# A mixer stage whose per-head reciprocal roots are made on all channels by one block-diagonal matrix

## The chip, the cores and the metric

The kernel runs on one core of a Trainium2 chip. The metric is the time of one execution on the device, in microseconds (us), less being better. The engines named below are TensorE (PE, with PEld for its weight loads), VectorE (DVE), ScalarE (ACT), GpSimd (POOL) and SyncE (SP), which issues the DMAs.

## The reference, cut to what matters

The whole network is four layers on an input of 8 x 512 x 256 in fp32: a mixer with an MLP, a mixture of experts, a gated delta attention and an expert-choice selection. The change touches only the mixer, in which each head of 16 channels is divided by its root mean square:

```python
def _rms(x, eps):
    return x * jax.lax.rsqrt(jnp.mean(x * x, axis=-1, keepdims=True) + eps)

q, k, v, a, g = jnp.split(x @ in_proj_w.T, 5, axis=-1)   # each reshaped to (B, S, 16 heads, 16)
q = _rms(q, EPS_FP32)
...
y = gate * (q * memory) + (1.0 - gate) * v               # memory: a decaying scan over k*v
return y.reshape(B, S, D) @ out_proj_w.T
...
x = x + RES_SCALE * _mixer(h1, in_proj_w, out_proj_w)
h2 = norm2_w * _rms(x, 1e-06)
return x + RES_SCALE * (jax.nn.silu(h2 @ fc_w.T) @ proj_w.T)
```

## The kernel before

The four stages follow one another; each has its own block, which begins when the one before has ended. The mixer, `stage_mixer`, works on one batch element (512 tokens x 256 channels) at a time. Channels are held on partitions in two halves (`KT` = 2), so a full tile is `[128, 2, 512]`, which the profile calls 128x1024; token-major tiles are `[128, 4, 256]`.

The loop is a hand-written software pipeline over `steps`: in one step each engine works on batch b (its attention half) and on batch a = b - 1 (its MLP half). The order in which each engine takes its pieces is written out by hand, and semaphores join them. Step 0 has no a, and the ninth step has no b.

PE in one step: `turn_h(b)` (L169, transposes), `project(b, 0, 6)` (L180), `turn_h2(a)` (L218), `project(b, 6, 10)`, `sum_heads(b)` (L189), `widen(a)` (L227, the MLP's first product), `spread_heads(b)` (L197 and L201), `narrow(a)` (L236, its second product), `project_out(b)` (L208).

DVE in one step: `second_norm(a)` (L402 to L409), `states(b)` (L362 to L374), `layer_norm(b + 1)` (L339 to L355), `head_norm(b)` (L381 and the shared helper `rsqrt`, L65 to L70), `mix(b)` (L388 to L393), `finish(a)` (L418).

ACT evicts PSUM: `scale_h` (L267), `parts` (L276 for the squares `q2`, L279 for the five projections), `squares` (L284), `scale_h2` (L289), `hidden` (L294), and last in a step the copy of the turned roots to `rqT` (L313). POOL adds `resm` (L321).

The roots of one batch take this path before the change. `sum_heads` makes the sums of squares per token and head by 8 products, in which slices of `q2` are the weights and the 16-column `head_sum` streams through; the result is 128 x 64 in PSUM bank 0. `head_norm` scales them and runs `rsqrt`, a bit trick with two integer operations and three Newton steps of three operations, on 128x64. `spread_heads` turns the roots to 16 x 512 (L197), ACT copies them to SBUF (L313), and two products with `head_spread` (L201) give each channel its root in banks 2 and 3. `mix` reads those in its first product (L388), and writes `y`, on which `project_out` waits.

Of the kernel before, what the change touches and what calls it, by code (L numbers as in the profile page):

```python
# [10 lines left out]
ALU = mybir.AluOpType  # L11
ACT = mybir.ActivationFunctionType
AX = mybir.AxisListType

P = 128
BATCH = 8
SEQ = 512
DIM = 256
KT = DIM // P
TT = SEQ // P  # L20
# [42 lines left out]
def rsqrt(eng, link, y, v, t):  # L63

    link(eng.tensor_scalar(t.bitcast(I32), v.bitcast(I32), 1, None, ALU.logical_shift_right))  # L65
    link(eng.tensor_scalar(y.bitcast(I32), t.bitcast(I32), -1.0, float(0x5F3759DF), ALU.mult, ALU.add))
    for step in range(3):
        link(eng.scalar_tensor_tensor(out=t, in0=y, scalar=-0.5, in1=y, op0=ALU.mult, op1=ALU.mult))
        link(eng.tensor_tensor(t, t, v, ALU.mult))
        last = eng.scalar_tensor_tensor(out=y, in0=t, scalar=1.5, in1=y, op0=ALU.add, op1=ALU.mult)  # L70
        if step < 2:
            link(last)
    return last
# [3 lines left out]
def stage_mixer(nc, io, x_in, x_out):  # L77
    HEADS, HDIM, CHUNK = 16, 16, 64
# [5 lines left out]
    Q_EPS = float(np.finfo(np.float32).eps)  # L84
# [5 lines left out]
    with ctx:  # L90
# [6 lines left out]
        n1 = sb("n1", [P, KT])  # L97
        n2 = sb("n2", [P, KT])
        ident = sb("ident", [P, P])
        head_sum = sb("head_sum", [P, KT, HEADS])  # L100
        head_spread = sb("head_spread", [HEADS, DIM])
        xin = sb("xin", [P, 3, TT, DIM])
        z = sb("z", [P, 2, TT, DIM])
        h = sb("h", [P, TT, DIM])
# [10 lines left out]
        prefix = sb("prefix", [P, KT, SEQ])  # L115
        mem = sb("mem", [P, KT, SEQ])
        y = sb("y", [P, KT, SEQ])
        rqT = sb("rqT", [HEADS, SEQ])
        hid = sb("hid", [P, FT, SEQ])
        sq = sb("sq", [P, TT, DIM])  # L120
        stats = sb("stats", [P, TT, 6])
# [1 line left out]
        rstd, r1, r2 = sb("rstd", [P, TT]), sb("r1", [P, TT]), sb("r2", [P, TT])  # L123
        vv, tmp, v2, tmp2 = (sb(n, [P, TT]) for n in ("vv", "tmp", "v2", "tmp2"))
        ss = sb("ss", [P, TT])
        rq, qv, tq = (sb(n, [P, TT * HEADS]) for n in ("rq", "qv", "tq"))
        two = sb("two", [P, 1])
        pace = sb("pace", [P, 1])
        ps = ctx.enter_context(nc.psum_tensor("mx_ps", [P, 8, 512], F32))
        names = ("w_in_loaded w_loaded x0 x1 x2 const_set h hTp hT proj proj_out q2 qs rq rqTp rqT rb y op mid ss resm h2 h2Tp h2T "  # L130
                 "fc hid mo out stored dv_norm dv_mem dv_q dv_y dv_h2").split()
        s = {n: sem(n) for n in names}
        x_sem = (s["x0"], s["x1"], s["x2"])
        W_IN_LOADS, W_LOADS = 3, 6
        block = ctx.enter_context(nc.Block())
        tok = lambda x, b: x[b].rearrange("(t p) d -> p t d", p=P)
        steps = [(b - 1 if b else None, b if b < BATCH else None) for b in range(BATCH + 1)]
# [1 line left out]
        @block.sync  # L139
        def _(sp):  # L140
            sp.dma_start(xin[:, 0, :, :], tok(x_in, 0)).then_inc(s["x0"], 16)
            for dst, src in [(ident[:, :], io["ident"]), (n1[:, :], io["norm1_w"]),
                             (w_in[:, :, :], io["in_projT"].rearrange("(k p) n -> p k n", p=P))]:
                sp.dma_start(dst, src).then_inc(s["w_in_loaded"], 16)
            sp.dma_start(xin[:, 1, :, :], tok(x_in, 1)).then_inc(s["x1"], 16)
            for dst, src in [(head_sum[:, :, :], io["head_sum"].rearrange("(k p) n -> p k n", p=P)),
                             (head_spread[:, :], io["head_spread"]), (n2[:, :], io["norm2_w"]),
                             (w_out[:, :, :], io["out_projT"].rearrange("(k p) n -> p k n", p=P)),
                             (w_fc[:, :, :], io["fcT"].rearrange("(k p) n -> p k n", p=P)),
                             (w_proj[:, :, :], io["projT"].rearrange("(k p) n -> p k n", p=P))]:  # L150
                sp.dma_start(dst, src).then_inc(s["w_loaded"], 16)
            sp.dma_start(xin[:, 2, :, :], tok(x_in, 2)).then_inc(s["x2"], 16)
            for b in range(BATCH):
                if b + 3 < BATCH:
                    sp.wait_ge(s["resm"], b + 1)
                    sp.dma_start(xin[:, b % 3, :, :], tok(x_in, b + 3)).then_inc(x_sem[b % 3], 16)
                sp.wait_ge(s["out"], b + 1)
                sp.dma_start(tok(x_out, b), outb[:, :, :]).then_inc(s["stored"], 16)
            sp.wait_ge(s["stored"], 16 * BATCH)

        @block.tensor
        def _(pe):
# [20 lines left out]

            def sum_heads(b):
                pe.wait_ge(s["q2"], KT * b + KT)
                pe.wait_ge(s["proj_out"], b * PARTS + 7)
                for t in range(TT):
                    for k in range(KT):
                        m = pe.matmul(ps[:, 0, t * HEADS:(t + 1) * HEADS], q2[:, k, t * P:(t + 1) * P],  # L189
                                      head_sum[:, k, :], start=(k == 0), stop=(k == KT - 1))  # L190
                m.then_inc(s["qs"], 1)

            def spread_heads(b):
                pe.wait_ge(s["proj_out"], b * PARTS + PARTS)
                pe.wait_ge(s["rq"], b + 1)
                for t in range(TT):
                    m = pe.transpose(ps[0:HEADS, 1, t * P:(t + 1) * P], rq[:, t * HEADS:(t + 1) * HEADS], ident[:, :])  # L197
                m.then_inc(s["rqTp"], 1)
                pe.wait_ge(s["rqT"], b + 1)
                for k in range(KT):  # L200
                    m = pe.matmul(ps[:, 2 + k, :], head_spread[:, k * P:(k + 1) * P], rqT[:, :], start=True, stop=True)  # L201
                m.then_inc(s["rb"], 1)

            def project_out(b):
                pe.wait_ge(s["y"], b + 1)
# [34 lines left out]
            for a, b in steps:  # L240
                if b is not None:
                    turn_h(b), project(b, 0, 6)
                if a is not None:
                    turn_h2(a)
                if b is not None:
                    project(b, 6, PARTS)
                    if b == 0:
                        pe.wait_ge(s["w_loaded"], 16 * W_LOADS)
                    sum_heads(b)
                if a is not None:  # L250
                    widen(a)
                if b is not None:
                    spread_heads(b)
                if a is not None:
                    narrow(a)
                if b is not None:
                    project_out(b)

        @block.scalar
        def _(act):  # L260
# [35 lines left out]
            for a, b in steps:  # L296
                if b is not None:
                    scale_h(b)
                if a is not None:
                    squares(a)  # L300
                if b is not None:
                    parts(b, 0, 6)
                if a is not None:
                    if a == 0:
                        act.wait_ge(s["w_loaded"], 16 * W_LOADS)
                    scale_h2(a)
                if b is not None:
                    parts(b, 6, PARTS)
                if a is not None:
                    hidden(a)  # L310
                if b is not None:
                    act.wait_ge(s["rqTp"], b + 1)
                    act.activation(rqT[:, :], ps[0:HEADS, 1, :], ACT.Copy).then_inc(s["rqT"], 1)  # L313

        @block.gpsimd
        def _(pool):
# [7 lines left out]
        def _(dve):  # L324
# [2 lines left out]
            dve.wait_ge(s["const_set"], 2)  # L327
            norm = Chain(dve, s["dv_norm"], 38)
            memory = Chain(dve, s["dv_mem"], 7)
            qnorm = Chain(dve, s["dv_q"], 11)  # L330
            gated = Chain(dve, s["dv_y"], 4)
            mid = Chain(dve, s["dv_h2"], 12)

# [44 lines left out]
            def head_norm(b):  # L378
                qnorm.start(b)
                dve.wait_ge(s["qs"], b + 1)  # L380
                qnorm(dve.tensor_scalar(qv[:, :], ps[:, 0, 0:TT * HEADS], 1.0 / HDIM, Q_EPS, ALU.mult, ALU.add))  # L381
                rsqrt(dve, qnorm, rq[:, :], qv[:, :], tq[:, :]).then_inc(s["rq"], 1)
                qnorm.end()

            def mix(b):
                gated.start(b)
                dve.wait_ge(s["rb"], b + 1)
                gated(dve.tensor_tensor(y[:, :, :], ch[Q][:, :, :], ps[:, 2:4, :], ALU.mult))  # L388
                gated(dve.tensor_tensor(y[:, :, :], y[:, :, :], mem[:, :, :], ALU.mult))
                gated(dve.tensor_tensor(y[:, :, :], y[:, :, :], ch[V][:, :, :], ALU.subtract))  # L390
                dve.wait_ge(s["proj_out"], b * PARTS + PARTS)
                gated(dve.tensor_tensor(y[:, :, :], y[:, :, :], ch[G][:, :, :], ALU.mult))
                dve.tensor_tensor(y[:, :, :], y[:, :, :], ch[V][:, :, :], ALU.add).then_inc(s["y"], 1)  # L393
                gated.end()
# [1922 lines left out]
def shape_constants():  # L2317

    f = np.float32
    head_sum = np.zeros((DIM, 16), f)  # L2320
    head_sum[np.arange(DIM), np.arange(DIM) // 16] = 1
    row, col = np.arange(P)[:, None], np.arange(P)[None, :]
    masks = np.zeros((P, 7, P), f)
    for l in range(7):
# [5 lines left out]
    for t in range(TT):  # L2330
# [5 lines left out]
    ident = np.eye(P, dtype=f)  # L2336
    krow = np.zeros((P, 1), f)
    krow[::32] = -1
    return dict(ident=ident, head_sum=head_sum, head_spread=head_sum.T, iota8=rows(8), masks=masks,
                keep128=keep128, ident4=np.broadcast_to(ident[:, None, :], (P, 4, P)), ones=np.ones((P, 1), f),  # L2340
                iota256=rows(SEQ // 2), before=before,
                lower=lower, krow=krow, keep_e=keep_e.reshape(P, -1), iota_b=rows(71))
# [40 lines left out]
```

## Time and profile before

| what | us |
|---|---|
| median of 3 runs | 4057.43 (4054.55 to 4061.96) |
| profiled execution, whole time | 4019.23 |
| its span | 4017.4 |
| PE busy in the span | 3306.8 (82%) |
| DVE busy | 2361.9 (59%) |
| ACT busy | 1368.9 (34%) |
| mixer, to its last store | 0 to about 514 |

The profiled execution is one execution, and every start and duration quoted below is of it. "Busy" counts the time in which an engine executes; the clock column is the clock granted to TensorE as a share of full speed, so 1.00 is 2.4 GHz and 0.50 is 1.2 GHz. An fp32 matmul of the program stands in the profile as two matmul instructions.

### The profile page before, as it was taken

What the parts mean: (1) busy time and instruction counts of PE and PEld (TensorE: products, weight loads), DVE (VectorE), ACT (ScalarE), POOL (GpSimd) and SP (SyncE); (2) the same over time, 40 slices, a digit from 0 to 9 for tenths busy, and PEclk for the clock granted to TensorE, in tenths of its full rate; (3) what the DMA queues carried; (4) which work ended last, traced back from release to release, by engine and by line L of the source; (5) the groups of instructions that cost most, each with busy time, mean ns of one, the idle gap of its engine ahead of it and who ended that gap; (6) DMA issues with size and microseconds to landing.
All of it is one profiled execution on the core that took longest, in us unless ns stands there. A gap on an engine that the chain in (4) does not pass through costs nothing. (4 is left out here: it accounts for less than half of the span.)

```text
span 4017.4 us, 53883 instructions
## 1 busy us (share of the span) xinstructions
PE 3306.8 (82%) x18986; PEld 2568.6 (64%) x18986; DVE 2361.9 (59%) x6068; ACT 1368.9 (34%) x2745; POOL 152.0 (4%) x149
## 2 busy tenths in 40 slices
PE   6999958888999999033698989898989889578777
PEld 3665534456999999022486868677676779455454
DVE  5555235545777777354668676766768584344442
ACT  2323212222444444000444453535344443022232
POOL 0000000023000000600000000000000000000000
PEclk8999969998999999555788889797979796578787
DMA  1000040024898987411201011010110100100000
GB/s 59 21 16 11 11 149 11 11 86 178 320 319 321 320 319 274 133 44 52 72 33 33 33 33 35 30 38 28 41 46 19 54 16 7 51 11 11 22 17 11
DMA packets 200529, 331.11 MB, mean 82 GB/s; under 512 B 29665, under 2 KB 154618, under 8 KB 199106
## 3 DMA queue, kind: packets, MB, share of 16 engines
q1 hardware_dynamic: 194114, 310.80, 22.3%
q0 software_dynamic: 6144, 16.79, 1.3%
q8 instruction: 159, 2.61, 0.3%
q14 instruction: 112, 0.92, 0.1%
HBM read 279.17 MB, written 48.37 MB: 82 GB/s over the span
## 5 line engine op out<-in xcount | busy, mean ns | idle before, releaser
L719 PE MATMUL ex_ps<-ex_xbT,ex_w 128*128 128x128 f32 x4544 | 532.4, 276 | 0.5 <-issue 0.5
L719 PEld LDWEIGHTS ex_ps<-ex_xbT,ex_w 128*128 128x128 f32 x4544 | 526.0, 193 | 4.5 <-issue 0.9
L1355 PE MATMUL de_ps<-de_hT,de_w 128*128 128x512 f32 x640 | 307.6, 639 | 26.4 <-DMA de_w<-in_w_kqv_dram 12.6
L799 ACT ACTIVATE ex_t<-ex_ps,ex_b 128x128 f32<-128x128 f32 x568 | 208.9, 368 | 336.5 <-PE ex_ps L719 320.0
L1355 PEld LDWEIGHTS de_ps<-de_hT,de_w 128*128 128x128 f32 x640 | 129.5, 207 | 187.7 <-issue 185.7
L663 PE MATMUL ex_ps<-ex_xT,ex_w 128*128 128x512 f32 x512 | 231.0, 607 | 14.6 <-DVE ex_gl L876 11.4
L876 DVE SCALAR_TENSOR_TENSOR ex_gl<-ex_ps,ex_b,ex_t 128x128 f32<-128x128 f32 (+1 forms) x316 | 123.6, 391 | 142.4 <-ACT ex_t L799 76.7
L663 PEld LDWEIGHTS ex_ps<-ex_xT,ex_w 128*128 128x128 f32 x512 | 97.6, 194 | 133.4 <-issue 113.6
L1712 DVE SCALAR_TENSOR_TENSOR de_ya<-de_kx,de_taps,de_ya 128x512 f32<-128x512 f32 x192 | 142.4, 750 | 49.8 <-ACT de_ya L1551 45.2
L876 DVE SCALAR_TENSOR_TENSOR ex_gm<-ex_ps,ex_b,ex_t 128x128 f32<-128x128 f32 (+1 forms) x316 | 121.7, 385 | 58.1 <-ACT ex_t L772 44.6
L180 PE MATMUL mx_ps<-mx_hT,mx_w_in 128*128 128x512 f32 x320 | 143.2, 604 | 8.3 <-ACT mx_hT L267 8.3
L1712 DVE SCALAR_TENSOR_TENSOR de_ya<-de_qx,de_taps,de_ya 128x512 f32<-128x512 f32 x192 | 142.8, 751 | 8.8 <-ACT de_ya L1551 2.6
L731 PE MATMUL ex_ps<-ex_w,ex_hid 128*128 128x256 f32 x568 | 134.5, 380 | 1.8 <-DVE ex_hid L901 1.8
L1076 PE MATMUL ga_ps<-ga_ident,ga_h 128*128 128x128 f32 x64 | 15.8, 427 | 143.2 <-DVE ga_h L1137 143.2
L1462 PE MATMUL de_ps<-de_PQ,de_DG 64*128 64x64 f32 x512 | 112.7, 417 | 16.6 <-ACT de_PQ L1615 16.6
L236 PE MATMUL mx_ps<-mx_w_proj,mx_hid 128*128 128x256 f32 x512 | 124.3, 408 | 0.0
L1462 PEld LDWEIGHTS de_ps<-de_PQ,de_DG 64*128 64x128 f32 x512 | 109.7, 327 | 20.4 <-ACT de_PQ L1615 20.4
L236 PEld LDWEIGHTS mx_ps<-mx_w_proj,mx_hid 128*128 128x128 f32 x512 | 105.0, 206 | 22.1 <-issue 5.8
L227 PE MATMUL mx_ps<-mx_h2T,mx_w_fc 128*128 128x512 f32 x256 | 114.7, 607 | 0.8 <-ACT mx_h2T L289 0.8
L2217 DVE TENSOR_REDUCE se_M<-se_ps 128x4 f32<-128x1024 f32 x64 | 75.3, 1219 | 65.9 <-PE se_ps L1981 65.7
L180 PEld LDWEIGHTS mx_ps<-mx_hT,mx_w_in 128*128 128x128 f32 x320 | 60.5, 193 | 81.4 <-issue 67.2
L898 DVE SCALAR_TENSOR_TENSOR ex_gl<-ex_gl,ex_gm 128x128 f32<-128x128 f32 (+1 forms) x316 | 105.4, 334 | 11.1 <-DVE ex_gl L896 0.2
(382 smaller groups left out, 6368.2 us busy)
## 6 DMA issues: line engine op xcount, KB each, us to landing
ex_w<-in_w_all_dram SPq DMA_DIRECT2D x144, 1024.0 KB, 7.1
ex_w<-in_w_all_dram SPq DMA_DIRECT2D x72, 512.0 KB, 7.9
de_w<-in_w_kqv_dram SPq DMA_DIRECT2D x80, 256.0 KB, 2.8
de_ab<-alpha_d SPq DMA_DIRECT2D x8, 2048.0 KB, 8.4
ex_xs_d<-ex_yb SPq DMA_DIRECT2D x71, 128.0 KB, 1.9
ex_xb<-ex_xs_d SPq DMA_DIRECT2D x71, 128.0 KB, 7.3
ex_ys_d<-ex_yb SPq DMA_DIRECT2D x71, 128.0 KB, 7.3
mx_xin<-in_x_dram SPq DMA_DIRECT2D x8, 512.0 KB, 3.9
```

The lines of the kernel that those rows point to most:

```text
L180: m = pe.matmul(ps[:, (n + 2) % 4, :], w_in[:, k, part * DIM + half * P:part * DIM + (half + 1) * P], hT[:, k, :], start=(k == 0), stop=(k ...
L227: m = pe.matmul(ps[:, 4 + f % 2, :], w_fc[:, k, f * P:(f + 1) * P], h2T[:, k, :], start=(k == 0), stop=(k == KT - 1))
L236: m = pe.matmul(ps[:, 6 + t // 2, t % 2 * DIM:(t % 2 + 1) * DIM], hid[:, f, t * P:(t + 1) * P], w_proj[:, f, :], start=(f == 0), stop=(f = ...
L663: m = pe.matmul(ps[:, bank, :], w[:, k, part * HID + c * P:part * HID + (c + 1) * P], xT[:, i % (LAG + 1), k, :], start=(k == 0), stop=(k ...
L719: m = pe.matmul(ps[:, n % 4, x * BLK:(x + 1) * BLK], w[:, k, part * HID + c * P:part * HID + (c + 1) * P], xbT[sx][:, k, :], start=(k == 0 ...
L731: m = pe.matmul(ps[:, 4 + sx, t * DIM:(t + 1) * DIM], hid[:, sx, c, t * P:(t + 1) * P], w2[s][:, c, :], start=(c == 0), stop=(c == HT - 1))
L799: act.activation(t1[:, n % 2, 0:BLK], ps[:, n % 4, 0:BLK], ACT.Identity, bias=b13[s][:, 0, n:n + 1]).then_inc(t1_ready, 1)
L876: dve.scalar_tensor_tensor(out=out[:, 0:width], in0=in0, scalar=b3[:, 1, n:n + 1], in1=t1[:, n % 2, 0:width], op0=ALU.add, op1=ALU.mult).t ...
L898: link2(dve.scalar_tensor_tensor(out=gl[:, 0:width], in0=gl[:, 0:width], scalar=1.0, in1=gm[:, 0:width], op0=ALU.add, op1=ALU.mult))
L1355: m = pe.matmul(ps[:, n % 2, :], w[:, g % SLOTS, k, n % 2 * P:(n % 2 + 1) * P], hT[:, k, :], start=(k == 0), stop=(k == KT - 1))
L1462: m = pe.matmul(ps[:, 2 + c % 2, hd * HALF:(hd + 1) * HALF], DG[0:HALF, c, hd, :], X11[0:HALF, c % 2, hd, :], start=True, stop=True, skip_ ...
L1712: m = dve.scalar_tensor_tensor(out=ya[:, n % 3, :], in0=xp(n)[:, i:i + SEQ], scalar=taps[:, col_of(n), i:i + 1], in1=ya[:, n % 3, :], op0= ...
```

## The change

The two constants `head_sum` and `head_spread` go, and one constant `head_block` comes: 128 x 128, with ones where row and column belong to the same head. `sum_heads` becomes two 128x512 products of `head_block` with `q2`, which leave the sum of its head at every channel, in banks 0 and 1. `head_norm` scales all 128x1024 values and runs `rsqrt` on 128x1024. `spread_heads`, the ACT copy, `rqT` and their semaphores go; `mix` takes the roots from SBUF.

```diff
@@ constants and waits @@
-            for dst, src in [(head_sum[:, :, :], io["head_sum"].rearrange("(k p) n -> p k n", p=P)),
-                             (head_spread[:, :], io["head_spread"]), (n2[:, :], io["norm2_w"]),
+            for dst, src in [(head_block[:, :], io["head_block"]), (n2[:, :], io["norm2_w"]),
-        rq, qv, tq = (sb(n, [P, TT * HEADS]) for n in ("rq", "qv", "tq"))
+        rq, qv, tq = (sb(n, [P, KT, SEQ]) for n in ("rq", "qv", "tq"))
-        W_IN_LOADS, W_LOADS = 3, 6
+        W_IN_LOADS, W_LOADS = 3, 5
@@ TensorE @@
             def sum_heads(b):
                 pe.wait_ge(s["q2"], KT * b + KT)
-                pe.wait_ge(s["proj_out"], b * PARTS + 7)
-                for t in range(TT):
-                    for k in range(KT):
-                        m = pe.matmul(ps[:, 0, t * HEADS:(t + 1) * HEADS], q2[:, k, t * P:(t + 1) * P],
-                                      head_sum[:, k, :], start=(k == 0), stop=(k == KT - 1))
+                pe.wait_ge(s["proj_out"], b * PARTS + 8)
+                for k in range(KT):
+                    m = pe.matmul(ps[:, k, :], head_block[:, :], q2[:, k, :], start=True, stop=True)
                 m.then_inc(s["qs"], 1)
-            def spread_heads(b):
-                pe.wait_ge(s["proj_out"], b * PARTS + PARTS)
-                pe.wait_ge(s["rq"], b + 1)
-                for t in range(TT):
-                    m = pe.transpose(ps[0:HEADS, 1, t * P:(t + 1) * P], rq[:, t * HEADS:(t + 1) * HEADS], ident[:, :])
-                m.then_inc(s["rqTp"], 1)
-                pe.wait_ge(s["rqT"], b + 1)
-                for k in range(KT):
-                    m = pe.matmul(ps[:, 2 + k, :], head_spread[:, k * P:(k + 1) * P], rqT[:, :], start=True, stop=True)
-                m.then_inc(s["rb"], 1)
...
-                if b is not None:
-                    spread_heads(b)
@@ ScalarE @@
-                if b is not None:
-                    act.wait_ge(s["rqTp"], b + 1)
-                    act.activation(rqT[:, :], ps[0:HEADS, 1, :], ACT.Copy).then_inc(s["rqT"], 1)
@@ VectorE @@
-                qnorm(dve.tensor_scalar(qv[:, :], ps[:, 0, 0:TT * HEADS], 1.0 / HDIM, Q_EPS, ALU.mult, ALU.add))
-                rsqrt(dve, qnorm, rq[:, :], qv[:, :], tq[:, :]).then_inc(s["rq"], 1)
+                qnorm(dve.tensor_scalar(qv[:, :, :], ps[:, 0:2, :], 1.0 / HDIM, Q_EPS, ALU.mult, ALU.add))
+                qnorm(rsqrt(dve, qnorm, rq[:, :, :], qv[:, :, :], tq[:, :, :]))
                 qnorm.end()
             def mix(b):
                 gated.start(b)
-                dve.wait_ge(s["rb"], b + 1)
-                gated(dve.tensor_tensor(y[:, :, :], ch[Q][:, :, :], ps[:, 2:4, :], ALU.mult))
+                gated(dve.tensor_tensor(y[:, :, :], ch[Q][:, :, :], rq[:, :, :], ALU.mult))
```

## Rows read from the trace of the kernel before

**Rows 1.** Busy time of the engines in one step of the mixer.
```profile
core 0: us, PE busy (x) PEld busy (x) DVE busy (x) ACT busy (x) POOL busy (x), PEclk, DMA share, GB/s
...
298.00:356.00 58.00, 56.36 (x194) 34.56 (x193) 30.89 (x86) 18.95 (x35) 2.35 (x1) 0.97 0.06 19
```
**Rows 2.** TensorE in order of time, one step: start, us, line, tiles, count.
```profile
260.74 1.85 PE L189 MATMUL mx_ps<-mx_head_sum,mx_q 128*128 128x16 f32 x16
262.44 13.98 PE L227 MATMUL mx_ps<-mx_h2T,mx_w_fc 128*128 128x512 f32 x32
276.26 0.60 PE L197 MATMUL mx_ps<-mx_ident,mx_rq 128*16 128x128 f32 x4
277.57 1.98 PE L201 MATMUL mx_ps<-mx_rqT,mx_head_spread 16*128 16x512 f32 x4 [0.72 <-ACT mx_rqT L313]
279.48 15.77 PE L236 MATMUL mx_ps<-mx_w_proj,mx_hid 128*128 128x256 f32 x64
295.09 3.62 PE L208 MATMUL mx_ps<-mx_w_out,mx_y 128*128 128x256 f32 x16
```
**Rows 3.** VectorE and ScalarE in order of time, same step.
```profile
268.28 0.21 DVE L381 TENSOR_SCALAR mx_qv<-mx_ps 128x64 f32<-128x64 f32 x1
...
276.46 0.60 ACT L294 ACTIVATE mx_hid<-mx_ps 128x512 f32<-128x512 f32 x1 [1.12 <-PE mx_ps L227]
...
279.59 1.22 DVE L388 TENSOR_TENSOR mx_y<-mx_ch,mx_ps 128x1024 f32<-128x1024 f32 x1 [8.30 <-PE mx_ps L201]
280.85 1.23 DVE L389 TENSOR_TENSOR mx_y<-mx_y,mx_mem 128x1024 f32<-128x1024 f32 x1
```
**Rows 4.** VectorE groups by line and shape over the mixer: mean ns of one.
```profile
L366 DVE TENSOR_TENSOR_SCAN mx_prefix<-mx_ch,mx_first_a 128x512 f32<-128x512 f32 x16 | 18.7, 1211 | 0.3
L369 DVE SCALAR_TENSOR_TENSOR mx_u<-mx_ch 128x1024 f32<-128x1024 f32 x8 | 9.8, 1225 | 23.4 <-ACT mx_ch L279 23.4
L362 DVE TENSOR_SCALAR mx_ch<-mx_ch 128x1024 f32<-128x1024 f32 x8 | 5.5, 688 | 11.0 <-ACT mx_ch L279 11.0
L66 DVE TENSOR_SCALAR mx_r<-mx_tmp 128x4 int32<-128x4 int32 x16 | 2.7, 170 | 0.5
L381 DVE TENSOR_SCALAR mx_qv<-mx_ps 128x64 f32<-128x64 f32 x8 | 1.7, 217 | 3.9 <-PE mx_ps L189 3.9
L66 DVE TENSOR_SCALAR mx_rq<-mx_tq 128x64 int32<-128x64 int32 x8 | 1.6, 195 | 0.3
```
**Rows 5.** A wait of TensorE in the mixer: us, times, longest.
```profile
PE mx_ps L208 <- DVE mx_y L393: 6.4, 1, 6.4
```
**Rows 6.** VectorE in order of time, step 0, then step 7.
```profile
46.95 0.21 DVE L381 TENSOR_SCALAR mx_qv<-mx_ps 128x64 f32<-128x64 f32 x1
...
60.64 1.23 DVE L393 TENSOR_TENSOR mx_y<-mx_y,mx_ch 128x1024 f32<-128x1024 f32 x1
...
436.42 0.22 DVE L381 TENSOR_SCALAR mx_qv<-mx_ps 128x64 f32<-128x64 f32 x1 [3.95 <-PE mx_ps L189]
```
**Rows 7.** TensorE's weight loads in order of time, around its restart in the last step.
```profile
479.55 1.57 PEld L218 LDWEIGHTS mx_ps<-mx_ident,mx_h 128*128 128x128 f32 x8 [7.53 <-DVE mx_h L409]
...
488.28 0.19 PEld L227 LDWEIGHTS mx_ps<-mx_h2T,mx_w_fc 128*128 128x128 f32 x1 [0.36 <-issue]
```
**Rows 8.** Two microseconds of step 0, columns as in rows 1 (clock, DMA share, GB/s last).
```profile
18.00:20.00 2.00, 1.31 (x2) 0.80 (x3) 0.00 (x0) 1.92 (x3) 0.00 (x0) 1.00 0.06 19
```
**Rows 9.** TensorE in order of time, the first output projection.
```profile
61.92 5.16 PE L208 MATMUL mx_ps<-mx_w_out,mx_y 128*128 128x256 f32 x16 [6.35 <-DVE mx_y L393]
```
**Rows 10.** Two stretches of the delta stage with much the same work.
```profile
2000.00:2050.00 50.00, 44.38 (x302) 42.88 (x303) 27.56 (x41) 28.85 (x56) 0.00 (x0) 0.60 0.00 1
2200.00:2250.00 50.00, 45.16 (x341) 43.47 (x340) 28.93 (x41) 26.95 (x53) 0.00 (x0) 0.74 0.01 1
```
**Rows 11.** SyncE's queue at the seam between mixer and experts.
```profile
514.28 0.36 SPq L158 DMA_DIRECT2D x_d<-mx_outb  x1
517.62 0.91 SPq L543 DMA_DIRECT2D ex_xin<-x_d  x2
```

More of the change, by code:

```diff
@@ L99, in stage_mixer @@
         ident = sb("ident", [P, P])
-        head_sum = sb("head_sum", [P, KT, HEADS])
-        head_spread = sb("head_spread", [HEADS, DIM])
+        head_block = sb("head_block", [P, P])
         xin = sb("xin", [P, 3, TT, DIM])
@@ L117, in stage_mixer @@
         y = sb("y", [P, KT, SEQ])
-        rqT = sb("rqT", [HEADS, SEQ])
         hid = sb("hid", [P, FT, SEQ])
@@ L129, in stage_mixer @@
         ps = ctx.enter_context(nc.psum_tensor("mx_ps", [P, 8, 512], F32))
-        names = ("w_in_loaded w_loaded x0 x1 x2 const_set h hTp hT proj proj_out q2 qs rq rqTp rqT rb y op mid ss resm h2 h2Tp h2T "
+        names = ("w_in_loaded w_loaded x0 x1 x2 const_set h hTp hT proj proj_out q2 qs y op mid ss resm h2 h2Tp h2T "
                  "fc hid mo out stored dv_norm dv_mem dv_q dv_y dv_h2").split()
@@ L329, in _ @@
             memory = Chain(dve, s["dv_mem"], 7)
-            qnorm = Chain(dve, s["dv_q"], 11)
+            qnorm = Chain(dve, s["dv_q"], 12)
             gated = Chain(dve, s["dv_y"], 4)
@@ L2319, in shape_constants @@
     f = np.float32
-    head_sum = np.zeros((DIM, 16), f)
-    head_sum[np.arange(DIM), np.arange(DIM) // 16] = 1
+    head_block = np.kron(np.eye(8, dtype=f), np.ones((16, 16), f))
     row, col = np.arange(P)[:, None], np.arange(P)[None, :]
@@ L2338, in shape_constants @@
     krow[::32] = -1
-    return dict(ident=ident, head_sum=head_sum, head_spread=head_sum.T, iota8=rows(8), masks=masks,
+    return dict(ident=ident, head_block=head_block, iota8=rows(8), masks=masks,
                 keep128=keep128, ident4=np.broadcast_to(ident[:, None, :], (P, 4, P)), ones=np.ones((P, 1), f),
```

## Prediction

> **What bounds the kernel now.** The change lies in the mixer alone, so I read the mixer and ask only at the end what its length does to the rest. Start with the busy times of one step. TensorE is busy 56.36 of 58.00 us at a granted clock of 0.97, VectorE 30.89 us, ScalarE 18.95 us [rows 1]. A step is as long as TensorE's queue, and the share to look for next is what TensorE does on behalf of the roots.
>
> Then the order of time on TensorE [rows 2]. Between `widen` and `narrow` stand the four transposes of the roots, a wait of 0.72 us for ScalarE's copy, and the four instructions that spread them: from 276.26 to 279.48. Next VectorE and ScalarE in the same step [rows 3]: the roots are started at 268.28, long before TensorE asks for them, and `mix` then starts only at 279.59, after 8.30 us of idling for the spread. Only once in the mixer does TensorE wait for `y`, for 6.4 us [rows 5], and that is step 0 [rows 9], which has no MLP half to lie beside the roots. So there are two different situations: seven steps (b = 1 to 7) bound by TensorE, and step 0 bound by VectorE's chain from the sums to `y`.
>
> The mixer's end is handed on in full: the last store is issued at 514.28, and the experts' first load, at 517.62, follows behind the block's end [rows 11].
>
> **Part by part, TensorE in steps 1 to 7.** The spread goes: 279.48 - 276.26 = 3.22 us a step. `narrow` can take the slot at once, since the last `hid` it needs is ready at 276.46 + 0.60 = 277.06 [rows 3] and is wanted only by the last 2 of the first 16 instructions, which at 15.61 us for 64 (295.09 - 279.48) comes 14 x 0.244 = 3.4 us after its start. `sum_heads` changes from 16 short instructions in 262.44 - 260.74 = 1.70 us to four 128x512 ones. `widen` shows those: 32 in 276.26 - 262.44 = 13.82 us, 0.432 each, so 1.73 us, 0.03 more [rows 2]. Net 3.19 us a step, 22.3 us for seven.
>
> **VectorE.** `head_norm` is now one scaling out of PSUM, two integer operations and nine products on 128x1024.
> - The nine have their twins in the trace: a three-operand product on 128x1024 takes 1225 ns [rows 4], and in a chain one starts 280.85 - 279.59 = 1.26 us after another [rows 3]. 9 x 1.26 = 11.32 us with the unrounded 1.258.
> - The integer ones have no twin of this size. The nearest below is the fp32 scaling, 688 ns; the integer operation itself goes from 170 to 195 ns when it grows from 4 to 64 elements, 0.42 ns an element, which carried on to 1024 gives 0.60 us [rows 4]. I take 0.69 and 0.03 for the gap: 1.44 us for both. The upper end is the dearest operation of the stage, the scan, 1.21 us for 512 columns, thus 2.42.
> - The scaling reads PSUM. Its small form takes 217 ns against 195 for the same shape out of SBUF [rows 4]. I take a product's 1.22 and 0.03; the bounds are 0.69 and 2.42.
>
> The sum is 1.25 + 1.44 + 11.32 = 14.0 us; `mix` after it is five products, 6.26 us to its end, 20.3 together. Upper bounds throughout add 2 x 1.73 + 1.20 = 4.7 us.
>
> The Trainium skill (VectorE: DVE Perf Modes, Why PSUM operands drop a tier) says that an fp32 operand in PSUM keeps a one-source operation at one element a cycle. The extra 22 ns of the row for 64 elements agree in direction; by the rule the scaling is the 1.22 that I took, and without it the sum would be 0.5 us shorter.
>
> In a steady step VectorE begins at 268.28, so `y` would be ready at 288.6. TensorE would reach `project_out` at 276.29 + 15.61 = 291.9. VectorE then arrives 3.3 us early, and the 11 us that it works more are covered by the part of `widen` still running and by `narrow`. If that cover went, each microsecond of overrun would cost one per step. Step 7 has more cover, because without a `layer_norm` its roots begin when the sums are there [rows 6]. `finish(a)` stands behind `mix` on VectorE and waits for `narrow`'s end anyway; `second_norm` waits for `project_out`. Nothing before `head_norm` on VectorE changes. ScalarE loses its copy, which was last in its step.
>
> **Step 0.** `head_norm` starts at 46.95, where `layer_norm(1)` lets it, and `y` was ready at 60.64 + 1.23 = 61.87 [rows 6]. It would be ready at 46.95 + 20.3 = 67.2: 5.35 us later, with nothing beside it. TensorE idles before that for some 27 us instead of two shorter gaps, and restarts at half clock. Before, the first output projection took 5.16 us against 3.62 in a steady step, 1.5 lost [rows 2, 9]. The last step shows a longer restart: from 479.55 to 488.28 weight loads run at the slower pace [rows 7], 8.7 us, and half of that, at most 4.4, is lost, 2.8 more than now. The other end is no extra loss. I take the middle, 1.5.
>
> The Trainium skill (TensorE: Matmul & The Clock Gate, What's actually happening) describes the clock as throttled by default and released by activity. The restart rows agree; by that rule alone, without a row for its length, the extra loss would have no size.
>
> **DMA and queues.** One small load replaces two on SP's queue, one issue fewer. The constants are needed by `sum_heads` of step 0 at about 38 us; from 18 us on the DMA engines are at 6% [rows 8]. Taken at nothing. POOL is not touched. The wait for the eighth eviction instead of the seventh is met before TensorE gets there, since the ninth and tenth projections lie between.
>
> **The sum.** -22.3 + 5.35 + 1.5 = -15.5 us. On the profiled execution, 4019.2 becomes 4003.7; that execution is 38 us under the median, by nothing the mixer shows, so I carry the difference over: 4057.4 - 15.5 = 4041.9 us.
>
> **Rivals.**
> - A: part of the freed slot stays. If `narrow` were held until all of `hid` is there (277.06 instead of 276.29), seven steps would lose 0.8 each: -10.1, 4047.3 us. Against it stands the order of its waits, one per slice of `hid`.
> - B: VectorE becomes the bound. With every unknown at its upper end, 4.7 us a step, step 0 loses 4.7 and steps 1 to 6 lose 4.7 - 3.3 = 1.4 each: -2.7, 4054.7 us. To end slower `head_norm` would have to pass 14.0 + 5.0 = 19.0 us, beyond those ends. Against it: the slope of the integer row.
> - C, the slower side: the clock of the later stages. Two stretches of the delta stage with similar work show 0.60 and 0.74 granted [rows 10]: 14 us more of half clock, up to 7 us lost. Everything behind the mixer shifts, so where the clock drops may shift with it. One more such place gives -8.5, two -1.5, four +12.5 us, 4069.9; it decides from the fourth on. One place better gives -22.5, 4034.9. For it: clock under 1 in many stretches there; against it: such stretches are set by the stage's own waits, which don't change.
> - D: the change doesn't do what it says. The second matmul form or the spread might not leave the queue; nothing in the code allows that, and it is left out of the chances.
>
> **How the numbers follow.** Forecast 70%, A 8%, B 6%, C worse 10% (half of it slower by over 0.2%), C better 6%. What a measurement of this kernel can tell from no change is 0.2%, 8.1 us. Faster: 70 + half of A + C better = 80%. Same: half of A, B, half of C worse = 15%. Slower 5%. The forecast's own bounds are -17 (no extra clock loss) and -14.2 (the long restart), widened by the runs' scatter of 4 us to either side; the range adds A, one better place of C and most of B, and runs from 4033 to 4055.
>
> **What would show it.** In the profile after: a steady step 3.2 us shorter; `narrow` directly behind `widen`; nine operations of 1225 ns and two of about 0.7 us per `head_norm`; TensorE not waiting for `y` in steps 1 to 7, with 2 to 4 us to spare; `y` of step 0 at about 67 us; the last mixer store at about 499. It is wrong if the integer operations on 128x1024 take well over 1.2 us, if TensorE waits for `y` in every step, or if the stages behind the mixer change length by more than some microseconds.

## The result, and the profile after

The changed kernel takes 4028.0 us (median of 4 runs, 4025.0 to 4030.9) against 4058.5 for the kernel before: a ratio of 0.9925, 95% interval 0.9908 to 0.9942. In a later round it was 0.9912 (0.9896 to 0.9929). The forecast was 4041.9 us in a range of 4033 to 4055. The direction was right; the gain was 30.5 us where 15.5 were forecast, and the time lies below the range. One execution is left out of the ratios below: of ten of the kernel before with its wait filled, nine took 4050 to 4060 us and one 6665.7.

First the seam between mixer and experts, SyncE's queue in the profile after, which answers to [rows 11].

```profile
484.10 0.36 SPq L155 DMA_DIRECT2D x_d<-mx_outb  x1
487.39 0.91 SPq L521 DMA_DIRECT2D ex_xin<-x_d  x2
```

The last store of the mixer is issued at 484.10 instead of 514.28. By then 30.2 us have been gained, as much as the medians show for the whole kernel (30.5). Next TensorE in order of time, one steady step, which answers to [rows 2].

```profile
227.97 3.62 PE L192 MATMUL mx_ps<-mx_w_out,mx_y 128*128 128x256 f32 x16
...
251.52 1.88 PE L185 MATMUL mx_ps<-mx_q,mx_head_block 128*128 128x512 f32 x4
253.24 13.90 PE L211 MATMUL mx_ps<-mx_h2T,mx_w_fc 128*128 128x512 f32 x32
266.97 13.98 PE L220 MATMUL mx_ps<-mx_w_proj,mx_hid 128*128 128x256 f32 x64
280.79 3.62 PE L192 MATMUL mx_ps<-mx_w_out,mx_y 128*128 128x256 f32 x16
```

A step takes 280.79 - 227.97 = 52.82 us. Before it took 57.91 (the same row of the kernel before starts at 237.18 and 295.09). Of the 5.09 us, the stretch between `widen` and `narrow` accounts for 3.22, as forecast. Most of the rest is in `narrow` (L220): the same 64 instructions on the same operands take 280.79 - 266.97 = 13.82 us, where they took 15.61 [rows 2]. That is 1.79 us a step, in a piece that no line of the diff touches. The last 0.09 us are in `widen` (13.73 instead of 13.82), less 0.02 in `sum_heads`.

Short stretches of the kernel before, in the steady step of [rows 2], tell why. The third number from the end is the clock granted to TensorE, and the count in the first brackets takes in every instruction that reaches into the slice.

```profile
279.00:280.00 1.00, 1.00 (x4) 0.49 (x3) 0.41 (x1) 0.00 (x0) 0.00 (x0) 0.96 0.00 0
280.00:281.00 1.00, 1.00 (x4) 0.74 (x4) 0.97 (x2) 0.00 (x0) 0.00 (x0) 0.50 0.00 0
...
282.00:283.00 1.00, 1.00 (x4) 0.82 (x3) 0.97 (x2) 0.00 (x0) 0.00 (x0) 0.50 0.00 0
283.00:284.00 1.00, 1.00 (x5) 0.83 (x5) 0.96 (x2) 0.00 (x0) 0.00 (x0) 0.84 0.00 0
284.00:285.00 1.00, 1.00 (x7) 0.87 (x6) 0.97 (x2) 0.00 (x0) 0.00 (x0) 1.00 0.00 0
```

TensorE is at work throughout, but right behind the turn and the spread of the roots the clock is at 1.2 GHz (0.50), from about 279.9 to 283.3, and a slice holds 4 instructions of `narrow` instead of 6 or 7. Half of those 3.4 us is lost, 1.7 of the 1.79. The trace has seven such falls, one in each of steps 1 to 7: `narrow` has the same 15.77 us in all of them. The same stretches after, and a whole step:

```profile
250.00:303.00 53.00, 52.08 (x173) 31.32 (x172) 42.10 (x88) 18.65 (x35) 2.35 (x1) 1.00 0.06 20
...
267.00:268.00 1.00, 1.00 (x6) 0.90 (x5) 1.00 (x1) 0.60 (x1) 0.00 (x0) 1.00 0.00 0
268.00:269.00 1.00, 1.00 (x6) 0.87 (x6) 0.97 (x2) 0.00 (x0) 0.00 (x0) 1.00 0.00 0
```

The step's mean clock is 1.00, where [rows 1] show 0.97, and VectorE is busy 42.1 of 53 us instead of 30.9 of 58. What VectorE and step 0 do after, in order of time; the first group answers to [rows 3], the last row to [rows 9]:

```profile
259.07 1.22 DVE L360 TENSOR_SCALAR mx_qv<-mx_ps 128x1024 f32<-128x1024 f32 x1
260.32 0.69 DVE L65 TENSOR_SCALAR mx_tq<-mx_qv 128x1024 int32<-128x1024 int32 x1
261.05 0.69 DVE L66 TENSOR_SCALAR mx_rq<-mx_tq 128x1024 int32<-128x1024 int32 x1
261.78 1.23 DVE L68 SCALAR_TENSOR_TENSOR mx_tq<-mx_rq 128x1024 f32<-128x1024 f32 x1
...
278.15 1.23 DVE L371 TENSOR_TENSOR mx_y<-mx_y,mx_ch 128x1024 f32<-128x1024 f32 x1
280.99 1.22 DVE L396 SCALAR_TENSOR_TENSOR mx_outb<-mx_ps,mx_resm 128x1024 f32<-128x1024 f32 x1 [1.61 <-PE mx_ps L220]
...
67.28 5.84 PE L192 MATMUL mx_ps<-mx_w_out,mx_y 128*128 128x256 f32 x16 [26.89 <-DVE mx_y L371]
```

`y` is ready at 278.15 + 1.23 = 279.38, and `project_out` begins at 280.79: 1.4 us to spare. In step 0 `y` comes at 67.2, and TensorE has waited 26.9 us for it.

The balance: seven steps give 7 x 5.09 = 35.6 us; step 0 costs 6.04 (the transposes behind its output projection start at 72.96 instead of 66.92); the last step is 0.6 shorter. That is 30.2 us.

### The profile page after: what moved, and what is told of

Its sections match the earlier page's. It is cut to its first block and busy times, and to the rows that moved or that the text cites. A ratio compares the mean times of both kernels' runs of the same rounds, so it can differ in the third digit from the quotient of the medians.

```text
span 4026.1 us, 53546 instructions
## 1 busy us (share of the span) xinstructions
PE 3272.6 (81%) x18826; PEld 2544.4 (63%) x18826; DVE 2449.1 (61%) x6068; ACT 1364.0 (34%) x2737; POOL 151.2 (4%) x149
## 3 DMA queue, kind: packets, MB, share of 16 engines
q1 hardware_dynamic: 193954, 310.84, 22.3%
## 5 line engine op out<-in xcount | busy, mean ns | idle before, releaser
L750 ACT ACTIVATE ex_t<-ex_ps,ex_b 128x512 f32<-128x512 f32 x64 | 43.9, 687 | 249.6 <-PE ex_ps L641 175.4
L220 PE MATMUL mx_ps<-mx_w_proj,mx_hid 128*128 128x256 f32 x512 | 111.8, 379 | 0.0
```

Source lines behind the costliest of these rows:

```text
L220: m = pe.matmul(ps[:, 6 + t // 2, t % 2 * DIM:(t % 2 + 1) * DIM], hid[:, f, t * P:(t + 1) * P], w_proj[:, f, :], start=(f == 0), stop=(f = ...
```

## The experiments

The hand-over, the start of the experts' first load, repeats well: 517.6 and 518.0 us in two profiles of the kernel before, 487.4 and 488.2 in two of the changed one, and at most 1.6 us apart for a kernel profiled twice. So one profile is enough to read an effect of several microseconds inside the mixer, while whole times scatter by 10 us and more. The theory is that the clock fell to half because of the old turn, wait and spread, which stood just ahead of `narrow`. Its rival is that `narrow` was slow for another reason, such as what stood ahead of it in the queue or what VectorE did beside it.

**The old stretch, put back as dead work** in the changed kernel.

```diff
+            def old(b):
+                pe.wait_ge(s["proj_out"], b * PARTS + PARTS)
+                for t in range(TT):
+                    m = pe.transpose(ps[0:HEADS, 2, t * P:(t + 1) * P], q2[:, 0, t * HEADS:(t + 1) * HEADS], ident[:, :])
+                m.then_inc(s["rqTp"], 1)
+                pe.wait_ge(s["rqT"], b + 1)
+                for k in range(KT):
+                    m = pe.matmul(ps[:, 2 + k, :], w_fc[0:HEADS, 0, k * P:(k + 1) * P], rqT[:, :], start=True, stop=True)
...
                     widen(a)
+                if b is not None:
+                    old(b)
...
                     hidden(a)
+                if b is not None:
+                    act.wait_ge(s["rqTp"], b + 1)
+                    act.activation(rqT[:, :], ps[0:HEADS, 2, :], ACT.Copy).then_inc(s["rqT"], 1)
```

> The changed kernel with the old stretch put back as dead work: four transposes to 16 partitions, ScalarE's copy of 16x512 with TensorE's wait for it, and two products of 16 rows; VectorE's work stays that of the changed kernel. Theory (clock): the step grows by 3.2 us for the stretch and by 1.8 us for a fall of the granted clock to 0.50 at the start of narrow, 7 x 5.0 = 35 us, 4063 us. Rival (narrow was slow before because of what VectorE did beside it, its first product out of PSUM above all): only 7 x 3.2 = 22.5 us, 4050.5 us, and clock 1.00.

The hand-over moved from 487.4 to 521.3 us, 33.9 later: 7 x 3.2 and about 6 x 1.8, for the 35 expected. The ratio to the kernel before was 1.0018 (1.0008 to 1.0029): with the stretch back, the gain is gone. The trace has six falls of the clock for seven steps, and the two kinds of step stand side by side. TensorE in order of time, and a microsecond of each `narrow` with its clock:

```profile
167.74 1.98 PE L196 MATMUL mx_ps<-mx_rqT,mx_w_fc 16*128 16x512 f32 x4 [0.72 <-ACT mx_rqT L307]
169.65 15.77 PE L230 MATMUL mx_ps<-mx_w_proj,mx_hid 128*128 128x256 f32 x64
171.00:172.00 1.00, 1.00 (x4) 0.82 (x3) 0.96 (x2) 0.00 (x0) 0.00 (x0) 0.50 0.00 0
185.25 3.62 PE L202 MATMUL mx_ps<-mx_w_out,mx_y 128*128 128x256 f32 x16
...
225.57 1.98 PE L196 MATMUL mx_ps<-mx_rqT,mx_w_fc 16*128 16x512 f32 x4 [0.72 <-ACT mx_rqT L307]
227.48 14.08 PE L230 MATMUL mx_ps<-mx_w_proj,mx_hid 128*128 128x256 f32 x64
229.00:230.00 1.00, 1.00 (x7) 0.87 (x6) 0.96 (x2) 0.00 (x0) 0.00 (x0) 1.00 0.00 0
241.40 3.62 PE L202 MATMUL mx_ps<-mx_w_out,mx_y 128*128 128x256 f32 x16
```

Same instructions, same neighbours, same VectorE work: 15.6 us where the clock fell, 13.9 where it didn't. Since VectorE does the changed kernel's work in both steps and the same instructions stand ahead in the queue, that leaves no room for the rival. It also shows that the stretch makes a fall likely, not certain; what decided it in the one step isn't known.

**The same place filled with full-array work.**

```diff
+            def fill_full(b):
+                pe.wait_ge(s["proj_out"], b * PARTS + PARTS)
+                for k in range(KT):
+                    m = pe.matmul(ps[:, 2 + k, :], head_block[:, :], q2[:, k, :], start=True, stop=True)
+                for k in range(KT):
+                    m = pe.matmul(ps[:, 2 + k, :], head_block[:, :], q2[:, k, :], start=True, stop=True)
...
                     widen(a)
+                if b is not None:
+                    fill_full(b)
```

> The changed kernel with eight more 128x512 matmul instructions on all 128 rows and columns, results unused, between widen and narrow of every step, where the turn and spread of the roots stood before. Theory (the old turn and spread used so little of the array that the clock granted to TensorE fell to 0.50 behind them, and narrow ran 1.8 us longer for it): a step grows by 8 x 0.432 = 3.5 us, the granted clock stays 1.00 through steps 1 to 7, narrow stays at 13.8 us; 4028.0 + 7 x 3.5 = 4052 us. Rival (narrow is slower whenever anything stands between it and widen, or whenever VectorE's products fall beside it): narrow goes back to 15.6 us, 4065 us.

The stretch from 90 to 400 us, and `narrow` in one of its steps:

```profile
90.00:400.00 310.00, 305.40 (x985) 180.10 (x984) 236.76 (x490) 100.12 (x182) 11.77 (x5) 1.00 0.05 16
...
280.25 13.98 PE L227 MATMUL mx_ps<-mx_w_proj,mx_hid 128*128 128x256 f32 x64
294.06 3.62 PE L199 MATMUL mx_ps<-mx_w_out,mx_y 128*128 128x256 f32 x16
```

Hand-over at 510.8, 23.4 us later for 24 expected; the mean clock from 90 to 400 us is 1.00, and `narrow` takes 13.8 us. Eight full-array instructions in the same place, 3.4 us against the old stretch's 3.2, cost their own length and no more. The whole time was 4049.6 us, ratio to the kernel before 0.9988 (0.9979 to 0.9998).

**One half of the stretch at a time**: only the two products on 16 rows, or only the transposes and the wait.

> The changed kernel with only the two products of 16 rows (four instructions, results unused) between widen and narrow; no turn, no wait. The changed kernel's mixer handed over to the experts at 487.4 us. Theory (it takes the whole quiet stretch of the old path, some 3.2 us of turn, wait and 16-row products, to bring the clock down): 7 x 1.73 = 12.1 us, hand-over at 499.5 us, clock 1.00 in steps 1 to 7. Rival (the products on 16 rows alone do it): 7 x 1.8 more, 512 us, clock at 0.50 behind each.

> The changed kernel with only the four transposes and TensorE's wait for ScalarE's copy between widen and narrow, as dead work. Theory (as for the spread alone): 7 x 1.3 = 9.2 us, hand-over at 496.6 us, clock 1.00 in steps 1 to 7. Rival (the idle wait is what the clock answers to): 7 x 1.8 more, 509 us.

`narrow` in one step of each kernel:

```profile
274.75 14.08 PE L225 MATMUL mx_ps<-mx_w_proj,mx_hid 128*128 128x256 f32 x64
...
272.24 14.08 PE L228 MATMUL mx_ps<-mx_w_proj,mx_hid 128*128 128x256 f32 x64 [0.72 <-ACT mx_rqT L305]
```

Hand-over at 501.0 and 497.1 us, in one profile each, without a fall in steps 1 to 7 in either. Neither the transposes with the 0.7 us wait nor the products on 16 rows brought the clock down alone; together they did. The halves are also shorter than the whole, so these runs don't tell whether it is the sum of their lengths or one of the kinds of work that counts.

**The kernel before with its wait filled.** Four instructions more in TensorE's queue, none fewer.

```diff
                 m.then_inc(s["rqTp"], 1)
+                for k in range(KT):
+                    m = pe.matmul(ps[:, 2 + k, :], w_in[:, k, 0:P], q2[:, k, :], start=True, stop=True)
                 pe.wait_ge(s["rqT"], b + 1)
```

> The kernel before with four more 128x512 full-array matmul instructions between the turn of the roots and the wait for ScalarE's copy, results overwritten. More work in TensorE's queue, nothing taken away. Theory (clock): the quiet stretch is broken, the fall of the clock goes, a step takes 0.85 us more for the filling that outlasts the copy and 1.8 us less in narrow: 7 x -0.95 = -6.6, 4052 us. Rival (no clock effect, or too little is filled): 7 x 0.85 = +6, 4064.5 us.

TensorE in order of time:

```profile
276.10 0.60 PE L197 MATMUL mx_ps<-mx_ident,mx_rq 128*16 128x128 f32 x4
276.54 1.88 PE L200 MATMUL mx_ps<-mx_q,mx_w_in 128*128 128x512 f32 x4
278.35 1.98 PE L203 MATMUL mx_ps<-mx_rqT,mx_head_spread 16*128 16x512 f32 x4
280.26 14.08 PE L238 MATMUL mx_ps<-mx_w_proj,mx_hid 128*128 128x256 f32 x64
294.18 3.62 PE L210 MATMUL mx_ps<-mx_w_out,mx_y 128*128 128x256 f32 x16
```

The stretch from 90 to 400 us, with its mean clock:

```profile
90.00:400.00 310.00, 305.40 (x1058) 183.18 (x1058) 168.23 (x477) 101.22 (x185) 11.77 (x5) 1.00 0.05 16
```

The falls of steps 1 to 7 are gone, `narrow` is back at 13.9 us, and a step takes 294.18 - 237.03 = 57.15 us with the added work, 0.76 less than without, for 0.95 expected. The mixer hands over at 514.3 instead of 517.6: 5.3 us gained in seven steps and 2.1 lost in step 0, where the added products run at half clock. That is half of the 6.6 us expected, and the whole time doesn't show it: 4055.5 us against 4052.3, ratio 1.0004 (0.9993 to 1.0016). The part behind the mixer took 3544.0 us in this kernel's profile, at the long end of what is told below, which may hide the rest. So the effect is shown inside the mixer, and as a measure for the whole kernel this edit brought nothing.

**How much cover is left on VectorE.** Four Newton steps in `head_norm`, three products more.

> The changed kernel with four Newton steps instead of three in head_norm: 3 x 1.26 = 3.8 us more on VectorE in every step. In the changed kernel y is ready at 279.4 us where project_out begins at 280.8, so the cover left is 1.4 us. Theory (VectorE is the next bound, 1.4 us away): step 0 loses 3.8 us, steps 1 to 6 lose 2.4 each, step 7 none: +18 us, hand-over at 505.5 us. Rival (the cover is the 3.3 us that was forecast): 3.8 + 6 x 0.5 = +7 us, 494.2 us.

The hand-over came at 509.4 us, 22.0 later. TensorE's waits in the mixer, and two output projections in order of time:

```profile
PE mx_ps L192 <- DVE mx_y L371: 44.2, 7, 30.7
...
239.16 5.41 PE L192 MATMUL mx_ps<-mx_w_out,mx_y 128*128 128x256 f32 x16 [2.26 <-DVE mx_y L371]
...
296.19 3.72 PE L192 MATMUL mx_ps<-mx_w_out,mx_y 128*128 128x256 f32 x16 [2.26 <-DVE mx_y L371]
```

The wait for `y`, once in the changed kernel, is there seven times: 30.7 us in step 0 and 2.26 us in each of steps 1 to 6. The 1.4 us of cover is confirmed: `project_out` starts 2.4 us later in each of the six steps, as expected. The 4 us over the 18 expected are the clock again: after the wait it fell in three of the six steps, and the projection behind such a fall takes 5.4 instead of 3.7 us, 5.1 us in all, while step 0 cost 1.8 us less than expected. The whole time was 4051.8 us, 0.9984 of the kernel before (0.9973 to 0.9996); three products of 1.2 us a step use up most of the change's gain.

**Step 0 shortened.** VectorE makes `layer_norm(1)` while it waits for the first projection.

```diff
                 if b is not None:
+                    if b == 0:
+                        layer_norm(1)
                     states(b)
-                    if b + 1 < BATCH:
+                    if 0 < b < BATCH - 1:
                         layer_norm(b + 1)
```

> The changed kernel, in step 0 only VectorE makes layer_norm(1) ahead of states(0), in the 11 us in which it waits for ScalarE's first projection, so that head_norm(0) starts when the sums are there, at about 40.4 instead of 46.95 us. Theory (step 0 is bound by VectorE's chain to y, nothing else): y comes 6.5 us earlier, 4028.0 - 6.5 = 4021.5 us. Rival (the input of batch 1 has not landed or the restart of TensorE eats it): under 3 us of gain, 4025 us or more.

`head_norm(0)` starts at 40.79 instead of 46.9, TensorE's wait for `y` falls from 26.9 to 20.5 us, and the hand-over comes at 481.2 us, 6.2 earlier. The ratio to the kernel before was 0.9903 (0.9886 to 0.9919). It was run again beside the changed kernel itself:

> The changed kernel with layer_norm(1) ahead of states(0), again, now beside the changed kernel itself. Theory: 6 us under the changed kernel (hand-over at 481.2 us). Rival (most of the 0.9903 measured before was scatter between chips and rounds): under 3 us.

> The changed kernel, unchanged, on the same chip and in the same rounds as the two that build on it. The mixer hands over at 487.4 us again with no fall of the clock in steps 1 to 7, and the ratio to the kernel before is again 0.9925, give or take 0.0015.

Changed kernel 4028.5 us, ratio 0.9912 (0.9896 to 0.9929); with `layer_norm(1)` first 4019.9, ratio 0.9900 (0.9879 to 0.9921). The hand-overs, 488.2 and 479.7, are 8.6 us apart, where it was 6.2 in the first pair. The intervals of the whole times overlap; the gain inside the mixer doesn't depend on them.

**The restarts.** On top of the edit above, dead full-array products keep the clock up in the two long waits; the cut shows only what is new.

```diff
+            def fill_gap(count):
+                for n in range(count):
+                    m = pe.matmul(ps[:, 2 + n % 2, :], head_block[:, :], q2[:, n % 2, :], start=True, stop=True)
...
                     sum_heads(b)
+                    if b == 0:
+                        pe.wait_ge(s["proj_out"], PARTS)
+                        fill_gap(22)
...
+                    if b is None:
+                        fill_gap(8)
                     turn_h2(a)
```

> The same with dead full-array products in TensorE's two long waits: 22 (44 instructions of 128x512, 19 us) while it waits for y of step 0, and 8 (16 instructions, 6.9 us) ahead of turn_h2 in the last step. Theory (what is lost at a restart is the clock alone): the first output projection takes 3.6 instead of 5.8 us, and the last step's transposes and widen 1.04 and 13.9 instead of 1.97 and 16.3 us: 2.2 + 3.3 us less, hand-over at 475.7 us. Rival (the restart costs something else, or the dead work gets in the way): no gain, 481 us or more.

```profile
40.08 19.05 PE L190 MATMUL mx_ps<-mx_q,mx_head_block 128*128 128x512 f32 x44
60.73 3.72 PE L196 MATMUL mx_ps<-mx_w_out,mx_y 128*128 128x256 f32 x16 [1.60 <-DVE mx_y L380]
...
443.33 14.00 PE L215 MATMUL mx_ps<-mx_h2T,mx_w_fc 128*128 128x512 f32 x32 [0.92 <-ACT mx_h2T L280]
```

TensorE in order of time: the first output projection takes 3.7 instead of 5.8 us, the last `widen` 14.0 instead of 16.3, and the hand-over comes at 475.7, as expected; beside the run without the dead products in the same round (479.7) that is 3.9 us, beside the earlier one (481.2) 5.5. The whole time is 4013.4 us, ratio 0.9879 (0.9861 to 0.9898), the best of all; its interval just touches that of the changed kernel in the same round and overlaps that of the run without the dead products.

**Behind the mixer.** The profiled execution of the kernel before took 4019.2 us, 38 under its median, and the one of the changed kernel 4027.9, on its median. From the experts' first load on, 3499.8 us in the one and 3538.7 in the other.

> The kernel before, unchanged, for a second profile of it. The profiled execution of before took 4019.2 us, its runs 4057; behind the mixer (from the experts' first load on) it took 3499.8 us, the changed kernel's profile 3538.7 us, with 60 us stalls of VectorE and ScalarE beside GpSimd's scatters. Theory (those stalls are common to both kernels and the first profile of before happened to be without them): the part behind the mixer takes 3530 us or more here, with such stalls, and the mixer again hands over at about 517.6 us with seven falls of the clock. Rival (the change made the later stages longer): about 3500 us again, and the experts' waits without them.

The second profile of the unchanged kernel before took 4052.4 us: hand-over 518.0, 3532.6 us behind it. All profiles but the first lie at 3531.8 to 3547.4 us there. Waits in the experts in the profile after, of the kind that the first profile of before has none of:

```profile
ACT ex_t L750 <- remote: 69.2, 2, 64.0
...
DVE ex_acc L883 <- remote: 59.7, 1, 59.7
```

They fall in the stretch in which GpSimd issues its scatters, in all the profiles but that one. In the second profile of before they are shorter than the expectation said (17.8 and 3.1 us), yet the difference lies in the same place: there SyncE stands still between its loads of `ex_xb` and its next loads of weights, from 955.5 to 989.8 us, where it did so from 954.9 to 956.5 in the first. All twelve other profiles have 34 to 47 us there, the first 1.6. What the engines wait for isn't named by the profile, and was not tried; that it isn't the change is shown by the kernel before having the long form too. It follows that the difference of the two first profiles (9 us) says nothing of the change, and that the sum had to be made on the mixer.

## Why the prediction came out as it did

**What bounds the kernel: right in kind, one reading missed.** The steady steps are bound by TensorE's queue and step 0 by VectorE's chain. But the view that began the argument gave a clock of 0.97 for a step in which TensorE never rests for more than a microsecond [rows 1]. I quoted it and did not ask where the missing 3% lay. It lay in one place in each step, behind the very instructions that the change removes.

**Removed on TensorE: 3.22 us a step, as forecast.** The block-diagonal products take 1.72 us for 1.73. Rival A did not occur: `narrow` follows `widen` at once.

**The step that failed: "Net 3.19 us a step, 22.3 us for seven".** It took `narrow` as untouched and carried its 15.61 us over into the changed order. That row was partly measured at half clock. In its place stands 13.82 us, and the runs with the stretch put back, halved and filled show that the stretch made the difference: 7 x 1.79 = 12.5 of the 14.7 us by which the forecast of the mixer fell short. The remainder is small terms: 0.09 us a step in `widen` (0.6 in all, its cause not looked into), 0.8 in the restart of step 0, 0.6 in the last step. A row at hand would have given the term: in the last step of before, which has no roots ahead of it, `narrow` is quick.

```profile
499.01 13.98 PE L236 MATMUL mx_ps<-mx_w_proj,mx_hid 128*128 128x256 f32 x64
```

**Cost on VectorE: right.** The scaling out of PSUM takes 1.22 us, the integer operations 0.69 each (the slope of the small ones would have given 0.60, the twin in fp32 0.69), the nine products 1.23; in the chain the whole runs from 259.07 to 273.12, 14.05 us for 14.0. The Trainium skill's rule on PSUM operands (VectorE: DVE Perf Modes, Why PSUM operands drop a tier) agrees: 1217 ns on average out of PSUM against 688 for the same shape out of SBUF.

**The cover: present, mis-sized.** Forecast 3.3 us to spare, measured 1.4. The difference of 1.9 is `narrow` again, 1.79 of it: the cover was priced with 15.61 us. It held, so rival B did not occur, but the run with a fourth Newton step shows how near it was.

**Step 0: right.** `y` 5.35 us later, forecast 5.35. For the restart I took 1.5 us more than before, the middle between two bounds; the output projection took 5.84 instead of 5.16, so 0.7.

**Rival C** named the clock, but in the delta stage and as chance. The clock did move, inside the mixer and in every step.

**Carrying the profiled execution over to the median** was right by luck: the difference between the two wasn't understood when it was written. My own sign of being wrong, later stages that change their length by more than some microseconds, did show in the first pair of profiles (39 us), and only the second profile of before tells that it isn't the change.

## What to carry to other kernels

A mean clock under 1.00 in a stretch where TensorE is always busy was a sum of short falls here: find each with short windows, and price the work behind it at full clock when the change takes away what stands before it. A duration may only be carried over together with the clock at which it was measured; the same line in another step is the quickest test. A short stretch of waiting and small products can cost more than its length: here 3.2 us of it cost 5.0 us a step. Taking it away may be worth more work on another engine: 11 us of VectorE time a step paid for 5.1 us of TensorE's.

## What the runs showed of the hardware

- The clock falls without a long idle. Transposes into 16 columns, 0.7 us of wait and 1.9 us of products on 16 rows, 3.2 us together, were followed by half clock in 7 of 7 steps of the kernel before and 6 of 7 with the stretch put back; either part alone, in none of 7, and 3.4 us of full-array products in its place, in none. Small products aren't needed for it: in the run with a fourth Newton step, a plain wait of 2.3 us behind `narrow` was followed by half clock in 3 of 6 steps, while the wait of 0.92 us behind the first transposes of every step never was. What the stretch and that wait have in common wasn't tried. The Trainium skill (TensorE: Matmul & The Clock Gate, A second HAM failure mode: psum-queue depth-cycling) describes short idles between groups of matmuls that bring the clock down without one long gap. This case agrees that no long gap is needed; a wait of 0.7 us with only the transposes ahead of it was not enough.
- More work can be less time: four instructions added to TensorE's queue shortened a step of the mixer from 57.91 to 57.15 us (the whole time shows no gain).
- Dead full-array products hold the clock over a wait of 20 us: with 19 us of it filled, the output projection behind it ran in 3.7 instead of 5.8 us.
- Whole times of this kernel carry a part behind the mixer that differed by up to 16 us between profiles of different kernels, and once by 33 us between two profiles of the same one. Those 33 us lie in one place, a stop of SyncE among the experts of 1.6 us in one profile and 34.4 in the other.
